# A graph kernel on one Trainium2 core: clearing the place of gathered rows behind the scores, and loading the words of first blocks behind a step's sums

## The reference, cut to what matters

```python
def agg(emb):
    a_input = jnp.concatenate([emb[head], emb[tail]], axis=-1)
    h = a_input @ fc_w.T + fc_b
    e = jnp.sum(h * rel_e, axis=-1)
    e = jnp.where(e > 0, e, LEAKY_SLOPE * e)
    m = jax.ops.segment_max(e, head, num_segments=N)
    ex = jnp.exp(e - m[head])
    denom = jax.ops.segment_sum(ex, head, num_segments=N)
    w = ex / denom[head]
    agg_emb = jax.ops.segment_sum(emb[tail] * w[:, None], head, num_segments=N)
    return agg_emb + emb
for _ in range(N_HOPS):            # two hops
    emb = agg(emb)
    emb = emb / jnp.maximum(jnp.sqrt(jnp.sum(emb * emb, axis=-1, keepdims=True)), EPS)
```

## Time and profile before

| | |
|---|---|
| median of 3 runs | 5893.11 us (5886.37 to 5901.3) |
| the profiled execution | 5902.71 us, span 5900.9 us, mean granted TensorE clock 0.846 |
| hop 1, 1155 to 2735 us | 1580 us, TensorE's records cover 1452 us |
| hop 2, 2817 to 4395 us | 1578 us, TensorE's records cover 1449 us |
| ahead of the hops, between them, behind them | 1155, 82 and 1506 us |

### The profile page before, as it was taken

How to read it: one execution, slowest core, us unless ns; L and a number is a source line. 1 busy time by engine, 2 the same in 40 slices (tenths; PEclk the granted TensorE clock), 3 DMA queues, 4 the chain that set the end, 5 groups by cost and what they waited for, 6 DMA issues and landing times. The chain is left out here.

```text
span 5900.9 us, 199689 instructions
## 1 busy us (share of the span) xinstructions
PE 4518.9 (77%) x53517; PEld 3713.5 (63%) x53518; DVE 3763.9 (64%) x11123; ACT 2406.1 (41%) x5659; POOL 2851.1 (48%) x2835
## 2 busy tenths in 40 slices
PE   3666666199999999996799999999974666666664
PEld 0001111098899898986798989999973555555553
DVE  8984887377777777777577777777773333333334
ACT  6201000066666666664466666666650111111111
POOL 0155666245555555552455555555532555555553
PEclk7668887599999999998899999999985766666666
DMA  7999999355555555553555555555531222222221
GB/s 284 404 413 410 413 415 415 109 146 144 145 150 145 145 150 146 144 149 69 143 150 147 146 148 147 148 147 149 147 84 42 50 50 50 50 49 51 50 50 39
DMA packets 489464, 949.05 MB, mean 161 GB/s; under 512 B 146548, under 2 KB 295693, under 8 KB 440209
## 3 DMA queue, kind: packets, MB, share of 16 engines
q1 hardware_dynamic: 397953, 799.51, 41.9%
q0 software_dynamic: 90336, 147.90, 11.2%
q10 hardware_dynamic: 1072, 0.31, 0.0%
HBM read 930.99 MB, written 14.32 MB: 160 GB/s over the span
## 5 line engine op out<-in xcount | busy, mean ns | idle before, releaser
L1486 POOL DMA_INDIRECT rows<-tab_d,stage_idx x1632 | 1611.4, 987 | 1620.2 <-PE ps_p L1532 592.7
L1515 PE MATMUL ps_t<-tab,hot_near 128*128 x8160 | 1146.7, 287 | 55.8 <-issue 27.4
L1868 POOL DMA_INDIRECT tab<-y_d,stage_src x768 | 727.7, 947 | 735.3 <-PE ps_all L1909 276.2
L1515 PEld LDWEIGHTS ps_t<-tab,hot_near 128*128 128x128 f32 x8160 | 1006.5, 193 | 105.5 <-issue 91.5
L1553 PE MATMUL ps_g<-rows,prob 128*128 128x65 f32 x6528 | 846.6, 273 | 171.1 <-issue 97.0
L1553 PEld LDWEIGHTS ps_g<-rows,prob 128*128 128x128 f32 x6528 | 793.8, 192 | 209.6 <-issue 165.7
L595 PE MATMUL ps_gate<-ring,h_sb 128*1 128x512 f32 x3072 | 561.2, 815 | 381.0 <-DMA ring<-w_ih 174.2
L1960 DVE TENSOR_SCALAR to_node<-wins_list,row_all 128x384 bf16<-128x384 bf16 x864 | 262.5, 324 | 865.4 <-remote 440.9
L1579 ACT ACTIVATE prob<-ps_p 128x512 f32<-128x512 f32 x816 | 486.9, 597 | 798.4 <-PE ps_p L1532 653.6
L1669 DVE TENSOR_SCALAR hot_near<-arena,node_code 128x640 f32<-128x640 bf16 x816 | 463.6, 568 | 400.8 <-PE ps_t L1515 254.3
L2022 ACT ACTIVATE arena<-ps_all 128x384 bf16<-128x384 f32 x432 | 211.7, 490 | 1172.3 <-PE ps_all L1896 531.3
(11 more groups left out here) (456 smaller groups left out, 6896.0 us busy)
## 6 DMA issues: line engine op xcount, KB each, us to landing
arena<-lo_d SPq DMA_DIRECT2D x816, 256.0 KB
ring<-w_ih SPq DMA_DIRECT2D x192, 1024.0 KB
ring<-w_hh SPq DMA_DIRECT2D x192, 1024.0 KB
arena<-code_d SPq DMA_DIRECT2D x816, 160.0 KB
arena<-list_lo_d SPq DMA_DIRECT2D x216, 128.0 KB
rows<-tab_d,stage_idx POOLq DMA_INDIRECT x1632
tab<-y_d,stage_src POOLq DMA_INDIRECT x768
rec_d<-arena,row_all POOLq DMA_INDIRECT x294
```

The source lines that it names most:

```text
L1486: pool.indirect_dma_start(out=rows[:, h * 4 + g, k, :], out_offset=None, in_=tab_d[hop], in_offset=bass.IndirectOffsetOnAxis(ap=stage_idx[ ...
L1515: mm = pe.matmul(ps_t[:, k * TW:(k + 1) * TW], lhsT=hot_near[:, p, at0 + b, :], rhs=tab[:, ds(at + b, 1), 0:TW].rearrange("p a c -> p (a c)"),
L1868: pool.indirect_dma_start(out=rows[:, g, k].rearrange("p j c -> p (j c)"), out_offset=None, in_=y_d, in_offset=bass.IndirectOffsetOnAxis(a ...
```

## The change

`gather` loses its wait for `kept` and its clearing matmul; they become `clear(g)`, which `body` calls behind `scores`, ahead of `spread`. And `blocks_from` loads the words at the first call of `number`, not at once. On TensorE that first call in a round is the one for `scores`, behind the `sums` of the round's first step; on ScalarE it is the one for the store to `acc`, behind `prob`, `prob_t` and `alpha`.

```diff
@@ -80,13 +80,15 @@
     at = i0 if each == 1 else i0 // each if isinstance(i0, int) else i0 >> (each // 2)
-    _, v = eng.bass.values_load_multi_w_load_instructions(
-        table[0:1, ds(at, words)], engines=(eng.engine,), min_val=0, max_val=2 ** 30 - 1,
-        skip_runtime_bounds_check_because="a word holds at most five numbers of six bits")
+    loaded = []
 
     def number(u, field):
+        if not loaded:
+            loaded.append(eng.bass.values_load_multi_w_load_instructions(
+                table[0:1, ds(at, words)], engines=(eng.engine,), min_val=0, max_val=2 ** 30 - 1,
+                skip_runtime_bounds_check_because="a word holds at most five numbers of six bits")[1])
         return eng.snap(eng.bass.s_assert_within(
-            (v[u // each] >> (u % each * (24 // each) + field * 6)) & 63, 0, top,
+            (loaded[0][u // each] >> (u % each * (24 // each) + field * 6)) & 63, 0, top,
@@ -1498,11 +1500,13 @@
-                        def gather(g, u, p, first, first_late):
+                        def clear(g):
                             wait(pe, kept, g)
                             pe.sem_inc(tick, 1)
                             pe.matmul(ps_t[:, 0:1], lhsT=zero_t[:], rhs=zero_t[:, 0:1], start=True, stop=True,
                                       skip_group_check=True)
+
+                        def gather(g, u, p, first, first_late):
                             with pe.bass.Fori(0, sweeps, 1, engines=(pe.engine,)) as w:
@@ -1559,6 +1563,8 @@
                             if stages[2]:
                                 scores(i - 2, u % 2, (u - 2) % 8, number(1))
+                            if stages[1]:
+                                clear(i - 1)
                             if stages[4]:
                                 spread(i - 4, u % 2)
```

## The result

The changed kernel takes 5946.7 us (median of 4 runs, 5939.7 to 5947.2), the kernel before beside it 5894.2 us: a ratio of 1.0083 with a 95% interval of 1.0071 to 1.0095, so 42 to 56 us slower. The forecast was 5925 us in a range of 5815 to 5990. The profiled execution took 5939.7 us (span 5936.9), 37 us more than the one of before; the two hops grew by more than that, and the parts around them came out 10 us shorter, for which no run shows a cause. From the gather's first matmul to its last it is 4419.3 - 1156.6 = 3262.7 us now; by the weight loads of the earlier trace rows it was 3215.3: +47 us.

The account below looks back on a forecast made before the run. TensorE was taken as the engine to shorten, a step taking 3.87 us against 3.38 with nothing late. Terms 159 - 56 - 61 - 10 = +32 us gave 5925 us by the median of 5893.1, range 5815 to 5990.

Parts of the forecast that it names:

- TensorE's step of 3.38 us: One TensorE step in the hops with nothing late, sums to sums; the average step was 3.87 us, the 0.49 between being waiting.
- the three kinds of waiting: TensorE's waits: 0.97 us before a round's first sums, 73.5 us for ScalarE's `prob`, 55.8 us before the gather.
- Late copies: ScalarE's late copy of gathered rows would hold up the moved clear in 331 steps, 0.48 us each: +159 us.
- my 0.48: Mean delay in us of the spread in a step whose copy of the gathered rows is late, charged in 331 steps.
- Absorbed: Idle time before the gather, put down to waiting for VectorE, would hide part of the late copies' cost: -56 us.
- rival 3: Nothing measurable: late copies overlap the `prob` and `hot_near` waits, load goes between gaps; within 18 us of 5893; chance 0.10.
- The gather's first load: With the clear gone from before the gather, its first weight load is covered: 0.11 us a step, -61 us.
- the 132 waits: Steps, of 408 in the first hop, where the gather waits for `hot_near` anyway, so the shorter start would not count.
- rival 2: Moving the clear's load saves nothing, the opening moves to the spread or isn't real: +93 us, 5986 us; chance 0.16.
- The words: Loading first-block words later starts a round's sums earlier but holds its scores back; 0.10 us a round, -10 us.
- Rival 1: ScalarE's copy is no longer late, or less so, through another phase of the engines: -71 us, 5822 us; chance 0.29.
- Signs to look for: Profile signs: clear idle 250 to 350 times, gather 1.24 us, idle before it a third, hop 1596 us instead of 1580.

Follow-up runs that it names:

- e4: Against the kernel before, only the wait for `kept` moved behind the scores, clearing matmul and words as before; second chip, within 0.15% of it and 38.5 us above e1.
- e1: Against the kernel before, the clear (wait and matmul) moved behind the scores, words loaded as before; 37 us faster on the second chip (kernel before 5285.5 us).
- e2: Against the kernel before, words loaded at first use on both engines, the clear left before the gather; 15 us faster on the second chip (kernel before 5285.5 us).
- e5: Changed kernel with GpSimd's second gather of a step released by VectorE's score of the next step; 5229.7 us on the second chip, the change 5232.6.
- e6: Changed kernel without the second GpSimd gather's wait for the turned probabilities; 5233.5 us on the second chip, the change 5232.6.
- e13: Against the kernel before, the clear between spread and turned probabilities, words at first use; third chip, 82 us slower, ratio 1.0138.
- e10: Kernel before with two spare ScalarE copies ahead of `rows` in every second step; third chip, first gather to last 175 us longer.

## Why the prediction was right, point by point

- **Bound and steps.** TensorE's step of 3.38 us and the three kinds of waiting held. The kernel got slower by the mechanism that was named, the clear waiting for a late `rows`, and by about the size: +52 us where +32 stood. That the size is so near is in part luck: two terms were off by 81 and 62 us in opposite directions, as follows.
- **Late copies, +159 us forecast, +240 measured.** The idle time before the clear (154.4 us, 266 times) is nearly the forecast's, but it is not the price. An interval between starts is: 240 / 266 = 0.90 us a late step. Three things were missing in my 0.48. The copies are later than before (median of the late ones 1.38 us behind the gather's end, 1.21 before the change). The idle time counts from the modelled end of the last score, 0.18 us behind its start, while without a wait the next matmul starts 0.03 us behind that start. And behind a clear that waited the spread starts 0.14 us later, not 0.03.
- **Absorbed, -56 us forecast, -118 measured.** The table has, first chip less second, -57 before the gather (185 to 93, less 125 to 90), -19 inside it, and -42 before the sums. The first is the term of the forecast, and its size is right, but not its reason. The prediction says of a late copy that "this costs TensorE nothing", and it takes the waits before the gather for waits for VectorE. Of their 55.8 us only 15.5 are VectorE's. In the late steps of the kernel before the gather starts 0.23 us (median) behind the clear instead of 0.03 and then takes 1.29 instead of 1.19 us to the sums: the register work behind a late `kept`, which the change covers with eight matmuls. The third are the waits for `prob`, 73.5 us before and 30.4 after, which I put into rival 3 and argued away ("a wait for `prob` starts from the turned probabilities, which the clear itself delays"). That was wrong: they shrank by more than half. This error and the one above nearly cancel. The four measured terms add up to 240 - 118 - 38.5 - 15 = +69 us, not 52: the other rows of the table take 5 us more, and the second chip's table falls by 66 us where its runs fall by 53.
- **The gather's first load, -61 us forecast.** The shorter start is there in every step: 0.08 us (1.35 to 1.27), on both chips, 63 us between e4 and e1. The forecast had 0.11, from 0.115 us a load, where 0.97 / 8 and 1.20 / 10 are 0.12 and leave 0.10. As it expected the gain does not all count, but for another reason than the 132 waits, behind which the earlier trace rows name no engine: 25 us go back at the round's turn, and 38.5 us are left. The Trainium skill (TensorE: Matmul & The Clock Gate, LDWEIGHTS) gives a load its time by its columns alone, and by that rule alone moving the clear gains nothing. e4 against e1 shows these 38.5 us, so the place counts too, and rival 2 is out.
- **The words, -10 us forecast, -15 measured** (e2), with their shape as told: 76 us less before the sums, 56 us more in the scores.
- **Rival 1** (no late copies, 71 us faster) is what the second chip shows: 53 us faster. I had it as a question of phase on the same chip. There the number did change, from 320 to 354 with the change, but upwards. (With the clear in the middle it is 624, on the third chip, for whose kernel before there is no trace.)
- **Signs to look for.** Idle before the clear 154.4 us in 266 cases (100 and more, 250 to 350 named); the gather at 1.27 us, not 1.24; idle before the gather less than half, not a third; a hop 24 us longer, not 16; before the sums of a round's first step some 0.4 us (45.7 us in 116 waits), as named.
- **The range.** Its lower end does not follow from the text: with the gain whole, 90 us, rival 1 comes to 5893 - 100 = 5793 us, not 5815. Nothing hung on it.

**Open** is why a chip delivers TensorE's signals late in 320 of 816 steps and another in none. What the profiles show is that it meets more than one engine at once (ScalarE and VectorE at 1292.29 and 1292.39) and SyncE's queue as well: 81 of these 816 issues take over 0.5 us on the first chip and 3 on the second. Its issues, in the kernel before on the first chip and then on the second (ns, least, median, most):

```profile
L1452 SPq DMA_DIRECT2D arena<-lo_d x816: 3/332/782, 1155.3 to 4351.1; - x164
```

```profile
L1452 SPq DMA_DIRECT2D arena<-lo_d x816: 276/333/599, 1152.1 to 4103.2; - x164
```

GpSimd's part in it (e5, e6) was not tried on a chip where it happens. One more thing differs, and it bears on every reading of the first chip: for the same kernel its trace holds 61245 records of semaphore updates and the second chip's 112365, in the first hop some 12 a us against 27. So on the first chip nearly half of them are missing, and the names of releasers there are less sure than the starts. The times of the change and of e1 to e13 all come with a span and a granted clock, so none is known to be from an execution without recording, and no run here shows whether the recording itself holds signals up.

## What to carry to other kernels

A wait that moves forward on the bounding engine has to be priced by how late its releaser comes in the steps where it is late, and from start to start; idle time before the waiting instruction told only two thirds of it here. Then look at what stands behind the wait: matmuls alone are cheap, but register and loop instructions that used to run ahead of the array come to lie open (e13, e10), even when the wait itself shows no idle time. And where a gain hangs on a signal being in time, compare more than one chip before trusting a sign: the same pair of kernels gave +0.8% on one and -1.0% on another.

## What was not expected of the hardware

- The same kernel takes 5894 and 5906 us on some chips and 5285 on two others, with the granted clock of the hops at 0.99 on both kinds. 245 us of it lie between the first copy of the gathered rows and the last (1163.5 to 4377.1 us on the first chip, 1160.4 to 4128.7 on the second), 367 in what comes behind the hops (spans of 5900.9 and 5285.8 us).
- Where signals come late, how often they do differs from kernel to kernel: 320 of 816 steps before, 354 with the change. With the clear in the middle it is 624, but on another chip of the same kind, so the order of the work and the chip are not told apart there.
- In the kernel before the clear sat idle for ScalarE's copy twice, 5.3 us, by the profile; yet in 163 of 816 steps the gather starts 0.64 us behind the end of that wait, at the pace of the register instructions between.
- With the clear between the spread and the turned probabilities the gather's start is as short as with the clear behind the scores (1.27 us), but the four turned probabilities take 0.64 us instead of 0.60 behind it: a one-column matmul lays part of an fp32 transpose's load open, though less than of the gather's.
